# Keeping VectorE's intermediate values of four steps in PSUM, in a four-layer megakernel on one Trainium2 core

## The reference

```python
# layer 0; the norm is over both axes of a batch's matrix
scale = (h @ Wsc + bsc)[:, None, :]; shift = (h @ Wsh + bsh)[:, None, :]      # h from an encoding of t
out = jax.nn.silu(scale * _layer_norm(x, gamma, beta) + shift)
out = out @ W_in + b_in
out = jax.nn.silu(scale * _layer_norm(out, gamma, beta) + shift)
x = out @ W_out + b_out + x
# layer 1: row norm with a scale and shift looked up by itok, attention of 16 heads of width 16
scores = jnp.where(src_mask, -jnp.inf, q @ k.T / 4 + attention_bias)
x = x + softmax(scores) @ v @ Wo + bo;  x = x + gelu2(ln(x) @ W1 + b1) @ W2 + b2
# layer 2: a stencil, with one-sided differences at the edges
df = -(_grad(A0*f, 1) + _grad(A1*f, 2)) + 0.5 * (_grad2(B0*f, 1) + _grad2(B1*f, 2) + 2 mixed terms of B2*f)
f = jnp.maximum(f + df * dt, 0.0)
# layer 3: norm, causal attention of 16 heads, MLP of 1024
out = f + g * (x2 - f)                                                         # x2: layer 3's result
```

## Time and profile before

| | us |
|---|---|
| median of 3 runs (3000.4 to 3002.53) | 3001.87 |
| the profiled execution, its own time | 3007.53 |
| its span, first to last instruction | 3006.2 |
| PE busy | 2697.6 (90%) |
| DVE busy | 2384.3 (79%) |
| ACT busy | 2351.0 (78%) |
| POOL busy | 1760.0 (59%) |

### The profile page before, as it was taken

The page is one execution under the profiler, slowest core; times in us unless marked ns, Lnnn a source line. Parts: engine busy times, 40 slices in busy tenths (PEclk is TensorE's granted clock), DMA queues, the critical chain, the costliest instruction groups (busy, mean ns, idle before and its releaser), DMA issues.

```text
span 3006.2 us, 61592 instructions
## 1 busy us (share of the span) xinstructions
PE 2697.6 (90%) x19916; PEld 2227.8 (74%) x19916; DVE 2384.3 (79%) x7946; ACT 2351.0 (78%) x5286; POOL 1760.0 (59%) x1736
## 2 busy tenths in 40 slices
PE   4667999999999999999999999999999999999866
PEld 3455787777777888777778778777787777777654
DVE  4667888888888888888888888988888888887633
ACT  1446888888888888888888888888888888888644
POOL 1556665666666666666666656666666656666311
PEclk7789999999999999999999999999999999999988
DMA  5223333333333333333333333333333333333010
GB/s 198 90 88 92 106 90 95 95 110 93 98 109 109 90 102 101 100 95 97 107 110 103 89 104 97 95 96 106 109 90 95 96 97 94 105 105 100 24 34 18
DMA packets 175089, 287.87 MB, mean 96 GB/s; under 512 B 44784, under 2 KB 98032, under 8 KB 174384
## 3 DMA queue, kind: packets, MB, share of 16 engines
q1 hardware_dynamic: 174768, 283.94, 32.1%
HBM read 174.64 MB, written 8.45 MB: 61 GB/s over the span
## 4 chain that ended last, share of the span: by engine, by line
PE 59%; DVE 16%; ACT 9%; issue 7%; POOL 7%; SPq 1%; DMA 1%; DVEq 0%; ACTq 0%; POOLq 0%
PE bank L955 15%; PE bank L948 13%; PE bank L976 8%; PE bank L925 7%; PE bank L933 5%; PE bank L968 4%; DVE PB L597 3%; ACT PB L786 3%; DVE PO L605 3%; PE bank L992 2%; POOL BT L369 2%; PE bank L993 2%; PE bank L940 2%; DVE FU L561 2%; ACT PH L792 2%
## 5 line engine op out<-in xcount | busy, mean ns | idle before, releaser
L786 ACT ACTIVATE PB<-PB,mx 128x256 f32<-128x256 f32 (+1 forms) x2048 | 840.8, 475 | 149.2 <-DVE mx L597 148.3
L605 DVE TENSOR_TENSOR PO<-bank,PH 128x384 f16<-128x384 f32 (+1 forms) x1024 | 633.1, 618 | 204.6 <-ACT PH L792 199.7
L792 ACT ACTIVATE PH<-bank 128x384 f16<-128x384 f32 (+1 forms) x1024 | 545.9, 534 | 150.1 <-PE bank L976 148.2
L369 POOL TENSOR_TENSOR BT<-BT,MN 128x1024 f32<-128x1024 f32 x256 | 559.3, 2195 | 105.3 <-DMA BT<-in_bias 105.0
L976 PE MATMUL bank<-ident,PB 128*128 128x128 f32 x3584 | 587.1, 281 | 27.8 <-DVE PO L605 15.7
L968 PE MATMUL bank<-Ks,Qs 96*128 96x512 f32 (+1 forms) x1024 | 527.4, 516 | 66.4 <-DVE mx L597 50.4
L976 PEld LDWEIGHTS bank<-ident,PB 128*128 128x128 f32 x3584 | 422.2, 143 | 109.2 <-ACT PB L786 55.1
L597 DVE CUSTOM_DVE_ANT_0 PB<-bank,caus 128x128 f32<-128x128 f32 (+1 forms) x1024 | 320.6, 350 | 135.8 <-PE bank L976 75.7
L597 DVE CUSTOM_DVE_ANT_0 PB<-bank,BT 128x256 f32<-128x256 f32 x1024 | 387.3, 415 | 20.4 <-PE bank L968 10.4
L992 PE MATMUL bank<-VP,PH 128*128 128x49 bf16 x3584 | 271.9, 187 | 15.4 <-DVE PO L605 14.0
L992 PEld LDWEIGHTS bank<-VP,PH 128*128 128x128 f16 x3584 | 208.9, 97 | 102.6 <-issue 55.8
(11 more groups left out here) (205 smaller groups left out, 5448.2 us busy)
## 6 DMA issues: line engine op xcount, KB each, us to landing
BT<-in_bias SPq DMA_DIRECT2D x256, 512.0 KB, 3.8
Qs<-QH SPq DMA_DIRECT2D x512, 64.0 KB, 2.4
Ks<-KH SPq DMA_DIRECT2D x1024, 32.0 KB, 2.0
Qs<-QU SPq DMA_DIRECT2D x256, 64.0 KB, 2.4
Ks<-KU SPq DMA_DIRECT2D x512, 32.0 KB, 2.0
XT<-in_xT SPq DMA_DIRECT2D x32, 256.0 KB, 2.9
X<-in_x SPq DMA_DIRECT2D x32, 256.0 KB, 2.9
AB<-ada_rows SPq DMA_DIRECT2D x32, 256.0 KB, 3.3
```

The lines of the kernel that those rows point to most:

```text
L369: G.op.tensor_tensor(v2(BT[k % 3]), v2(BT[k % 3]), MN[:, :].unsqueeze(1).broadcast_to([128, 2, 512]), ALU.add).then_inc(g_bt, 1)
L605: V.op.tensor_tensor(PO[i][:, 0:w], bP[h][:, 0:w], PH[i][:, 0:w], ALU.subtract).then_inc(v_low, 1)
L786: S.op.activation(o, o, ACT.Exp, scale=-1.0, bias=mx[u.layer][:, c:c + 1]).then_inc(a_exp, 1)
L792: S.op.activation(PH[i][:, 0:w], bP[h][:, 0:w], ACT.Copy).then_inc(a_high, 1)
```

## The change

Three things. First, DVE's intermediate values stay in PSUM: in layer 0 centring writes bF, scaling reads and writes bF, the two noise scalings read bF and write FU, tanh writes bF and the gate reads it; in the context the reciprocal is written to column 49 of each 64-column group of bV instead of a tile rc; in the stencil r is built in bM; in the output the sum is written to bT_. Second, the stencil's 16 matmuls no longer begin with the start flag, so they add onto what DVE wrote, and L725 goes away. Third, in layer 0 two one-column instructions become tensor_scalar with two pointer scalars, and the sign change L552 goes away (POOL's rstd multiplies by -1 instead). Three waits ask for a later event: the first pv matmul of a pair for the end of L618, c1 for the end of L730, t3 for the end of L753. The table P is written in another form with the same numbers, so that all pieces keep their ticks.

```diff
             def all_sum(s, sem, n):
                 V.op.tensor_copy(g, bF[:, 0:2]).then_inc(sem, 1)
                 V.wait_ge(sem, n + 4)
-                V.op.scalar_tensor_tensor(out=v, in0=g[:, 0:1], scalar=g[:, 0:1], in1=g[:, 1:2],
-                                          op0=ALU.mult, op1=ALU.subtract).then_inc(sem, 1)
-                V.wait_ge(sem, n + 5)
-                V.op.tensor_scalar(v, v, -1.0, None, ALU.mult).then_inc(sem, 1)
+                V.op.tensor_scalar(v, g[:, 0:1], g[:, 0:1], g[:, 1:2], ALU.mult, ALU.subtract).then_inc(sem, 1)
             def all_center(x, s, sem):
-                V.op.scalar_tensor_tensor(out=FU[:, :], in0=x[:, :], scalar=s[:, 8:9], in1=gT[:, :],
+                V.op.scalar_tensor_tensor(out=bF[:, :], in0=x[:, :], scalar=s[:, 8:9], in1=gT[:, :],
             def all_scale(s, b, sem, n):
-                V.op.scalar_tensor_tensor(out=FU[:, :], in0=FU[:, :], scalar=s[:, 11:12], in1=bT[:, :],
+                V.op.scalar_tensor_tensor(out=bF[:, :], in0=bF[:, :], scalar=s[:, 11:12], in1=bT[:, :],
                 for d in range(2):
-                    V.op.tensor_scalar(half(FU, d), half(FU, d), hs[:, d, b:b + 1], hb[:, d, b:b + 1],
+                    V.op.tensor_scalar(half(FU, d), half(bF, d), hs[:, d, b:b + 1], hb[:, d, b:b + 1],
             def all_gate(sem):
-                V.op.scalar_tensor_tensor(out=FU[:, :], in0=FY[:, :], scalar=1.0, in1=FU[:, :],
+                V.op.scalar_tensor_tensor(out=FU[:, :], in0=bF[:, :], scalar=1.0, in1=FU[:, :],
...
-                        V.op.reciprocal(rc[:, 0:8].unsqueeze(2), pv[:, :, 48:49]).then_inc(v_pvn, 1)
+                        V.op.reciprocal(pv[:, :, 49:50], pv[:, :, 48:49]).then_inc(v_pvn, 1)
...
-                            rc[:, 0:8].rearrange("p (a h) -> p a h", a=4).unsqueeze(3).broadcast_to([128, 4, 2, 16]),
+                            pv[:, :, 49].rearrange("p (a h) -> p a h", a=4).unsqueeze(3).broadcast_to([128, 4, 2, 16]),
...
-                p, m, w1, r = AA
+                p, m, w1, r = *AA[0:3], bM
...
-                    V.op.tensor_tensor(r[:, :], bM[:, :], r[:, :], ALU.add).then_inc(v_s, 1)
-                    V.wait_ge(v_s, n + 14)
                     V.op.scalar_tensor_tensor(out=r[:, :], in0=r[:, :], scalar=dtb[:, b:b + 1], in1=f[:, :],
...
-                    V.op.tensor_tensor(y[:, :], bT_[:, :], y[:, :], ALU.add).then_inc(v_o, 1)
+                    V.op.tensor_tensor(bT_[:, :], bT_[:, :], y[:, :], ALU.add).then_inc(v_o, 1)
-                    V.op.scalar_tensor_tensor(out=y[:, :], in0=y[:, :], scalar=gtb[:, b:b + 1], in1=X[b % 5][:, :],
+                    V.op.scalar_tensor_tensor(out=y[:, :], in0=bT_[:, :], scalar=gtb[:, b:b + 1], in1=X[b % 5][:, :],
...
-                    S.wait_ge(v_n2, 11 * b)
-                    S.op.activation(FY[:, :], FU[:, :], ACT.Tanh).then_inc(a_n1, 1)
+                    S.op.activation(bF[:, :], FU[:, :], ACT.Tanh).then_inc(a_n1, 1)
...
-                            T.wait_ge(v_pvn, 3 * (D // 2 - 1) + 2)
+                            T.wait_ge(v_pvn, 3 * (D // 2 - 1) + 3)
...
-                        T.wait_ge(v_s, 16 * (b - 1) + 14)
+                        T.wait_ge(v_s, 15 * (b - 1) + 15)
...
-                                last = T.op.matmul(half(bM, q), Gm[:, c:c + 128], half(w, k), start=(n == 0), stop=(n == 3))
+                                last = T.op.matmul(half(bM, q), Gm[:, c:c + 128], half(w, k), start=False, stop=(n == 3),
+                                                   skip_group_check=True)
...
-                    T.wait_ge(v_o, 2 * (b - 2) + 1)
+                    T.wait_ge(v_o, 2 * (b - 2) + 2)
```

More of the change, by code:

```diff
@@ L40, with begin @@
 S3 = 160
+BEGIN1 = {}
+BEGIN3 = {}
+def begin(layer, b):
+    if layer == 1:
+        return PERIOD * b + BEGIN1.get(b, 0)
+    return PERIOD * b + S3 + BEGIN3.get(b, 0)
 P = {
@@ L59 @@
     "s_pm": 71, "s_r": 71, "s_rp": 72, "s_re": 78, "s_ha": 71, "s_w": 78, "s_p2": 78, "s_mm": 81, "s_f": 95,
[L61 to L66, removed]
+    "coef": -16, "coefs": -27,
[4 rows of a table added]
+}
+LATE = {
+    "m3", "m3_rstd", "m3_norm", "t3", "t3_out", "y3", "q3", "q3_out", "q3_lo", "k3", "k3_out", "k3_lo", "v3",
+    "v3_out", "v3_hi", "v3_sub", "v3_mid", "v3_lo", "c3", "c3_out", "o3", "m4", "m4_rstd", "m4_norm", "m4_b", "t4",
+    "t4_out", "w3", "w3_out", "w3_gelu", "w4", "out", "st_out",
 }
@@ L84, in build @@
 def build(nc, A, OUT, scr, NB=32):
-    starts = sorted((PERIOD * b + s + 4 * n, layer, b, n) for b in range(NB) for layer, s in ((1, 0), (3, S3))
-                    for n in range(8))
+    starts = sorted((begin(layer, b) + 4 * n, layer, b, n) for b in range(NB) for layer in (1, 3) for n in range(8))
     units = [Unit(D, layer, b, n) for D, (_, layer, b, n) in enumerate(starts)]
@@ L89, in build @@
     number = {(u.layer, u.b, u.n): u.D for u in units}
-    ticks = range(min(P.values()) - 20, PERIOD * NB + max(P.values()) + 20)
+    ticks = range(min(P.values()) - 120, begin(3, NB - 1) + max(P.values()) + 40)
+    batch_of = {layer: {begin(layer, b): b for b in range(NB)} for layer in (1, 3)}
     def at(t, piece):
-        b, rest = divmod(t - P[piece], PERIOD)
-        return [b] if rest == 0 and 0 <= b < NB else []
+        b = batch_of[3 if piece in LATE else 1].get(t - P[piece])
+        return [] if b is None else [b]
     def unit_at(t, piece):
@@ L324, in rstd @@
             def rstd(v, out, sem, n):
-                G.op.tensor_scalar(out, v, EPS, 1.0, ALU.add, ALU.mult).then_inc(sem, 1)
+                G.op.tensor_scalar(out, v, -1.0, EPS, ALU.mult, ALU.add).then_inc(sem, 1)
                 G.wait_ge(sem, n + 1)
@@ L541, in all_stats @@
                 V.wait_ge(sem, n + 2)
-                V.op.scalar_tensor_tensor(out=s[:, 7:8], in0=s[:, 6:7], scalar=s[:, 6:7], in1=s[:, 7:8],
-                                          op0=ALU.mult, op1=ALU.add).then_inc(sem, 1)
+                V.op.tensor_scalar(s[:, 7:8], s[:, 6:7], s[:, 6:7], s[:, 7:8], ALU.mult, ALU.add).then_inc(sem, 1)
             def all_sum(s, sem, n):
@@ L703, in stencil @@
                 for b in at(t, "s_rp"):
-                    n = 16 * b
+                    n = 15 * b
                     V.wait_ge(v_s, n + 1)
@@ L711, in stencil @@
                 for b in at(t, "s_re"):
-                    ends(er, X[b % 5], r, 16 * b + 3)
+                    ends(er, X[b % 5], r, 15 * b + 3)
                 for b in at(t, "s_w"):
-                    n = 16 * b
+                    n = 15 * b
                     V.wait_ge(g_s, 5 * b + 3)
@@ L733, in third @@
                 for b in at(t, "m3"):
-                    V.wait_ge(v_s, 16 * b + 16)
+                    V.wait_ge(v_s, 15 * b + 15)
                     V.wait_ge(a_m3, 2 * b)
@@ L841, in scalar @@
                 for b in at(t, "n2_tanh"):
-                    S.wait_ge(v_n2, 11 * b + 10)
-                    S.op.activation(FY[:, :], FU[:, :], ACT.Tanh).then_inc(a_n2, 1)
+                    S.wait_ge(v_n2, 10 * b + 9)
+                    S.op.activation(bF[:, :], FU[:, :], ACT.Tanh).then_inc(a_n2, 1)
                 for b in at(t, "x1_norm"):
```

48 lines of the change are left out of this document (24 added, 24 removed), and 4 rows, old and new, of the table P.

## The result

The changed kernel takes 2920.9 us (median of four runs, 2917.4 to 2922.6), the kernel before 3002.2 beside it: ratio 0.973, 95% interval 0.971 to 0.975. The forecast was 2940 in a range of 2923 to 2972. The profiled execution has a span of 2921.3 us, against 3006.2.

A forecast was written before the change was run, and what follows sets the result against it. PE bounds the kernel (busy 90%), so DVE counts only where PE waits. From 3007.5 us profiled, less 50 (steady batches) and 12 (start), 2945.5; 5.7 less as median: 2940 us, range 2923 to 2972.

The forecast's parts named there:

- What blocks: DVE instructions with two SBUF tensors, or tensor_scalar SBUF to SBUF, wait for POOL; those with a PSUM operand don't.
- Steady batches: Middle of the kernel: 86.1 us a batch falls towards the 84.16 of one nearly unblocked batch in the trace; 50 us gained.
- Instructions removed: L725 and L552 go, but DVE has 12 us to spare per batch: 0 in the steady part.
- Dearer instructions: L565 and L730 lose the quick form, 0.8 us of DVE a batch, covered by 1.5 us: nothing on the path.
- writing to PSUM: DVE writing PSUM or working in place there: taken as 0; bound at the dear end a second pass, 0.69 us.
- later waits: First pv matmul, c1 and t3 wait for later events, with 1, 15 and 13 us of cover: nothing.
- Start: 30 to 355 us: 11 us from unblocked L561 and L565, 1 from other forms held there; 12 us gained.
- Tail: After 2770 us: neither norm runs there, so nothing gained.
- C: Blocks stay because a PSUM operand frees nothing: 3002 us less 1 to 6 for removed instructions; chance 0.04.
- D: Slower: dear PSUM writes make DVE the bound; at 0.5 us for each of about 35 instructions 3098 us; chance 0.06.
- B: Larger gain: other waits for DVE, such as L669's, shrink by 8 us and start gives 22: 2922 us; chance 0.08.
- Half-clock stretches: Five 5 us stretches of PE at partly 1.2 GHz behind idle PE, 8.5 us; none expected between 400 and 2650 us.

The follow-up runs named there:

- b_scale: Kernel before, with only layer 0's affine step writing its result to PSUM bank bF, where the two noise scalings read it: 2975.8 us.
- b_layer0: Kernel before, with all of layer 0's intermediate values (centering, affine step, tanh) in PSUM bank bF and no other part of the change: 2959.1 us.
- a_noscale: Changed kernel, with layer 0's affine step writing FU in SBUF again and the noise scalings reading FU: 2948.5 us.
- b_nomask: Kernel before, with POOL's mask addition cut to one column, so it computes something else; DVE's instructions untouched: 2931.4 us, one run.
- a_dummy: Changed kernel, with one unused 128x512 DVE addition more per batch, ahead of the scaling by dt: 2919.1 us.
- b_lay_ctx: Kernel before, with layer 0's values and the context's reciprocals in PSUM, without the stencil, output or small-step parts: 2936.7 us.
- a_noctx: Changed kernel, with the context's part undone: reciprocals go to the small SBUF tile rc again: 2927.8 us.
- b_stencil: Kernel before, with the stencil's part alone: r in PSUM bank bM, PE accumulating onto it, one addition less: 2995.8 us.

## Why the prediction was off, point by point

*What blocks.* Right: DVE instructions with two SBUF inputs, or tensor_scalar from SBUF to SBUF, are held by POOL, and a PSUM source frees them. Shown from DVE's side by b_scale, b_layer0 and a_noscale, from POOL's by b_nomask.

*Steady batches*, "Against the free batch's 84.16": the step that failed. I took that batch for the shortest that the change could reach, and sized the term at 50 us; it measured 72. The batch lacked the block at the scalings, but it was not free: the earlier trace rows show one place of it only. The chain around the stencil was held there as in every batch, and the change touched it and two waits more (stencil, small steps, context, output). That gave another 0.59 us, by 28 batches 17 us. The other 5 us I gave away by taking 50 where the 28 periods stood 55 above 28 free batches.

*Instructions removed*, "0 in the steady part": the reason, DVE's idle time, holds for the addition (a_dummy), but not for the part as a whole. An idle engine doesn't show that none of its instructions is on a path: undoing the stencil's part cost 0.16 us a batch, the small steps 0.16.

*Dearer instructions*, *writing to PSUM*, *later waits*: right. A write to PSUM or in place costs 6 ns (L561 746, L576 752), far from the bound of a second pass. PE's waits after the change show no DVE context step, and the context's multiplication (L633, before L618) never takes over 290 ns.

*Start*: the sum is right, 12.6 us against 12, its make-up is not, so the hit is luck in good part. I gave 11 us to layer 0's steps and 1 to all else. Up to the third batch's stencil b_layer0 gains 6.0 us, b_lay_ctx 9.7, the changed kernel 12.6. *Tail*: 1.7 us longer, and between 155 and 163 us in the variants; not explained.

*Rivals.* C and D are out. B, 2922 us, came to the size, and partly by luck: its 22 us at the start didn't come (12.6). It was right that other waits for DVE shrink. The one for L669 fell from 0.23 to 0.14 us a batch, and a_noctx brought the 0.09 back, so they are the context's. I weighed B down since "those rows sit in the free batch as well". They did, and the change shortened them in that batch too.

*Half-clock stretches*: none after between 400 and 2650 us, as said. Where they stood, in the kernel before and in the variants, the batch took 87.5 us or more: b_stencil has four there and b_scale three, b_layer0 and a_noscale have none.

## What to carry to other kernels

An undisturbed period found in the trace bounds what one block costs, not what the kernel can reach: list every wait of the busiest engine in that period, and ask which of them the change also touches. The longest wait of the busiest engine was worth nothing here while a second chain ran past it; before moving work to close a wait, follow back what the next wait of that engine hangs on, and shorten both. To keep DVE clear of POOL, give its instruction a source in PSUM, or let POOL start its instruction once DVE is through.

## What the runs showed of the hardware

- A PSUM target alone doesn't free a DVE instruction from POOL (b_scale, L561: up to 2687 ns with two SBUF inputs; in b_layer0, with one, at most 759).
- The block works both ways: POOL's mask addition took 2.58 us beside a DVE subtraction from SBUF and 2.13 alone, and DVE's subtraction 1.51 beside POOL and 0.69 alone.
- A held instruction need not be large: the one-column L542 took up to 2177 ns in the kernel before (least 219), and L618 with 128 columns 2269 (median 294).
- tensor_scalar over 512 columns takes 691 ns from PSUM (L743) and 426 from SBUF (L730); the kernel was faster with the slower form.
